# Attention scores from queries and keys in two float32r parts, one score product of 50 rows per head, maxima in pairs

## What is computed

```python
qkv = (x @ qkv_w + qkv_b).reshape(Bx, Tx, 3, H, HD).transpose(2, 0, 3, 1, 4)
q, k, v = (qkv[0], qkv[1], qkv[2])
...
q = _apply_rotary(q, rope)
k = _apply_rotary(k, rope)
scale = HD ** (-0.5)
scores = jnp.einsum('bhqd,bhkd->bhqk', q, k) * scale
causal_mask = jnp.triu(jnp.ones((Tx, Tx), dtype=bool), 1)
scores = jnp.where(causal_mask, -jnp.inf, scores)
attn = jax.nn.softmax(scores, axis=-1)
out = jnp.einsum('bhqk,bhkd->bhqd', attn, v)
```

## Time and profile before

| | |
|---|---|
| median of 3 runs | 3247.66 us |
| lowest and highest | 3235.09 and 3250.77 us |
| span of the profiled execution, first to last instruction | 3061.1 us |
| PE, PEld busy | 2843.4 (93%), 1573.9 (51%) us |
| DVE busy | 2242.9 us (73%) |
| ACT busy | 1779.3 us (58%) |
| POOL busy | 1253.7 us (41%) |

### The profile page before, as it was taken

One profiled execution on the slowest core, in us unless ns is written; L12 is line 12 of the kernel. 1 busy time (PEld: TensorE's weight loads), 2 busy tenths in 40 slices (PEclk: granted clock), 3 DMA queues, 4 the chain that ended last, 5 costly groups with the idle time before them and its releaser, 6 DMA issues.

```text
span 3061.1 us, 61038 instructions
## 1 busy us (share of the span) xinstructions
PE 2843.4 (93%) x22500; PEld 1573.9 (51%) x22500; DVE 2242.9 (73%) x5047; ACT 1779.3 (58%) x2736; POOL 1253.7 (41%) x1557
## 2 busy tenths in 40 slices
PE   7888799999999999989999999987999999999997
PEld 4433333333433334433333333323888999999997
DVE  7888788888888888899998888822393225566477
ACT  2422466666566665656665566665556666666533
POOL 6766311213521114521114765554305753443176
PEclk9999899999999999999999999998999999999998
DMA  4854323313312322412323535245336765665486
GB/s 163 209 142 106 110 56 65 66 42 76 101 39 56 66 63 59 109 43 37 66 63 91 141 94 123 89 129 152 117 93 204 233 202 175 187 183 173 136 238 193
DMA packets 290690, 359.05 MB, mean 117 GB/s; under 512 B 65404, under 2 KB 243212, under 8 KB 290140
## 3 DMA queue, kind: packets, MB, share of 16 engines
q1 hardware_dynamic: 259516, 279.94, 33.8%
q0 software_dynamic: 26112, 71.34, 7.7%
q10 hardware_dynamic: 4768, 3.88, 0.5%
HBM read 206.25 MB, written 139.21 MB: 113 GB/s over the span
## 4 chain that ended last, share of the span: by engine, by line
PE 49%; ACT 13%; DVE 10%; POOL 7%; issue 7%; DMA 2%; ACTq 1%; POOLq 0%; SPq 0%; DVEq 0%
ACT P L1643 13%; PE PB L1165 10%; PE PB L1092 8%; PE PB L1181 7%; DVE mx L1460 6%; PE PB L1062 6%; PE PB L1039 6%; PE PB L1075 5%; POOL x_slots L1846 4%; PE PB L1106 2%; PE PB L1150 2%; ACTq L1652 1%; POOL yg L1859 1%; PE PB L1129 1%; POOL x_slots L1838 1%
## 5 line engine op out<-in xcount | busy, mean ns | idle before, releaser
L1460 DVE TENSOR_REDUCE mx<-PB 128x1 f32<-128x512 f32 (+3 forms) x2560 | 1406.9, 603 | 214.6 <-PE PB L1039 135.6
L1643 ACT ACTIVATE P<-PB 128x1024 f32<-128x1024 f32 (+3 forms) x1280 | 1095.4, 894 | 643.3 <-PE PB L1075 629.3
L1039 PE MATMUL PB<-KO,QO 64*128 64x512 bf16 (+3 forms) x2560 | 762.0, 353 | 61.5 <-DVE mx L1460 51.5
L1092 PE MATMUL PB<-P,V 128*17 128x512 f32 (+3 forms) x5120 | 599.2, 540 | 11.8 <-POOL P L1797 11.7
L1062 PE MATMUL PB<-QO,KO 64*128 64x512 bf16 (+3 forms) x2560 | 546.8, 353 | 60.0 <-ACT P L1643 33.0
L1039 PEld LDWEIGHTS PB<-KO,QO 64*128 64x128 bf16 x2560 | 203.5, 94 | 718.0 <-DVE mx L1460 533.0
L1075 PE MATMUL PB<-QO,KO 34*128 34x512 bf16 (+3 forms) x2560 | 520.0, 351 | 0.6 <-DMA QO<-nh 0.4
L1797 POOL TENSOR_SCALAR_AFFINE_SELECT P<-P 128x256 f32<-128x256 f32 x512 | 208.6, 414 | 678.8 <-ACT P L1643 673.1
L1165 PE MATMUL PB<-xT,ws 128*128 128x128 f32 x3432 | 433.7, 277 | 7.1 <-ACT xT L1726 7.0
L1165 PEld LDWEIGHTS PB<-xT,ws 128*128 128x128 f32 x3432 | 408.2, 193 | 9.7 <-ACT xT L1726 9.7
L1571 DVE TENSOR_TENSOR haT<-sl,PB 64x128 f32<-64x128 f32 x350 | 101.4, 290 | 411.8 <-ACT sl L1735 407.3
(11 more groups left out here) (178 smaller groups left out, 3218.7 us busy)
## 6 DMA issues: line engine op xcount, KB each, us to landing
xq<-x_slots SPq DMA_DIRECT2D x286, 128.0 KB, 2.8
qk_parts<-pt SPq DMA_DIRECT2D x192, 128.0 KB, 2.4
KO<-qk_parts SPq DMA_DIRECT2D x192, 128.0 KB, 4.1
y_slots<-yo SPq DMA_DIRECT2D x191, 128.0 KB
QO<-qk_parts SPq DMA_DIRECT2D x64, 256.0 KB, 3.4
rden<-rden_rows SPq DMA_DIRECT2D x256, 64.0 KB
y_slots<-mx SPq DMA_DIRECT2D x95, 128.0 KB
v_rows<-vst SPq DMA_DIRECT2D x16, 544.0 KB, 4.0
```

The costliest lines, as they stand in the source:

```text
L1039: mm = pe.matmul(PB[:, bank, 0:n], QO[half, k3, j, 128 * t:128 * t + 128], KO[half, k3, j, 512 * kc:512 * kc + n], start=True, stop=True)
L1092: mm = pe.matmul(PB[32 * j:32 * j + 17, 7, c0:512], V[:, g % 2, kt, 17 * j:17 * j + 17], P[:, pbuf(g, i, j // 2), j % 2, 0:n], start=kt == ...
L1460: dve.tensor_reduce(mx[:, j, t, kc:kc + 1], PB[:, u.bank[item], 0:n], AX.X, ALU.max).then_inc(s["mx"], 1)
L1643: act.activation(P[:, pbuf(g, i, p), :, 0:n], PB[:, 2 * p:2 * p + 2, 0:n], ACT.Exp, scale=0.25).then_inc(s["exp"], 1)
```

## The change

Queries and keys are kept as two f32 parts, "high", rounded to float32r by ScalarE, and "low", what GpSimd's one subtraction leaves. The third part, `pe_` and its steps are gone. In `QO` and `KO` a head has 48 rows of products (high by high, high by low, low by high), and two rows more for the negated maximum and the ones. "sa" and "sb" become one product "s" over 50 rows of half of the array; "max" is one product over 48 rows. Both read float32r. The tensors take the same room as before. In a step the maxima are issued two at a time, one on each half. The masking products stay in bf16.

```diff
+HIGH, LOW = 0, 1
 LOADS = [(z, 64 * odd + row, odd, k, n) for odd in (0, 1)
-         for z, row, k, n in ((0, 0, 0, 2), (0, 32, 0, 2), (1, 0, 0, 1), (1, 16, 0, 1), (1, 32, 1, 1), (1, 48, 1, 1))]
-LOADS += [(z, 64 - 64 * odd + row, odd, k, 1) for odd in (0, 1) for z, row, k in ((0, 0, 2), (0, 16, 0), (1, 0, 0), (1, 16, 2))]
+         for z, row, k, n in ((1, 0, HIGH, 2), (0, 16, HIGH, 2), (1, 32, HIGH, 1), (0, 0, HIGH, 1))]
+M_ROW = 48
 NL = len(LOADS)
...
-        if k == 4 and c > 1:
-            o("lo", c - 2)
+        if k == 4 and c > 0:
+            o("lo", c - 1)
...
         quota = (want - done) // 2 * 2
         at = done
         ahead = order[n + 1] if n + 1 < len(order) else None
+        o("s", g, i, 2)
+        o("s", g, i, 3)
+        o("exp", g, i, 1)
         if len(pend) == 2:
             values(*pend.pop(0))
-        maxima(at + (quota + 2) // 4)
-        o("sa", g, i, 3)
-        o("sa", g, i, 2)
         maxima(at + quota // 2)
         if ahead:
-            o("sa", *ahead, 0)
-            o("sa", *ahead, 1)
-        o("sb", g, i, 3)
-        o("sb", g, i, 2)
-        o("exp", g, i, 1)
+            o("s", *ahead, 0)
+            o("s", *ahead, 1)
+            o("exp", *ahead, 0)
         if i >= 2:
             pumped(pumps)
-        maxima(at + quota // 2 + (quota + 2) // 4)
-        if ahead:
-            o("sb", *ahead, 0)
-            o("sb", *ahead, 1)
         maxima(at + quota)
-        if ahead:
-            o("exp", *ahead, 0)
         send_rows()
...
-    parts_d = scratch("qk_parts", [B, H, 2, 3, HD, T], BF16)
+    parts_d = scratch("qk_parts", [B, H, 2, 2, HD, T])
...
-        QO = A("QO", [128, 3, 4, T], BF16)
+        QO = A("QO", [128, 3, 2, T], F32)
         ko_at = A.at
-        KO = A("KO", [128, 3, 4, T], BF16)
+        KO = A("KO", [128, 3, 2, T], F32)
         v_at = A.at
...
+        QR, KR = QO[:, :, :, :].bitcast(F32R), KO[:, :, :, :].bitcast(F32R)
...
+                    q.wait_ge(s["c_p"], 3)
+                    for k in (0, 2):
+                        for odd in (0, 64):
+                            sync.dma_start(KO[odd + M_ROW:odd + M_ROW + 2, k], KO[odd + 32:odd + 34, 2]).then_inc(s["l_one"], 16)
...
-                    q.wait_ge(*lo_done[c])
+                    q.wait_ge(s["p_low"], c + 1)
-                        for k in range(3):
+                        for k in (HIGH, LOW):
                             for half in (0, 1):
                                 sync.dma_start(parts_d[b, :, z, k, 8 * half:8 * half + 8, tok:tok + 512],
                                                pt[w][:, k, 2 * z + half, :]).then_inc(s[f"w_p{w}"], 16)
...
-                    sync.dma_start((QO, KO)[z][row:row + 16 * n, k3, odd:4:2, :],
+                    sync.dma_start((QO, KO)[z][row:row + 16 * n, k3],
                                    parts_d[b, h0 + odd:h0 + 4:2, z, k:k + n].rearrange("h k d t -> (k d) h t")
...
-                    half = slice(64 * (j % 2), 64 * (j % 2) + 64)
-                    mm = pe.matmul(PB[:, bank, 0:n], QO[half, k3, j, 128 * t:128 * t + 128], KO[half, k3, j, 512 * kc:512 * kc + n],
-                                   start=True, stop=True)
+                    half, rows = slice(64 * (j % 2), 64 * (j % 2) + 64), slice(64 * (j % 2), 64 * (j % 2) + M_ROW)
+                    mm = pe.matmul(PB[:, bank, 0:n], QR[rows, k3, j // 2, 128 * t:128 * t + 128],
+                                   KR[rows, k3, j // 2, 512 * kc:512 * kc + n], start=True, stop=True)
                     if kc == t // 4:
...
-                elif name == "sa":
+                elif name == "s":
                     g, i, j = at
                     c, kt = STEPS[i]
                     k3, p = (g + 2) % 3, j // 2
                     n, c0 = nb(i)
                     q0 = 512 * c + c0
-                    rows = slice(64 * (j % 2), 64 * (j % 2) + 64)
+                    rows = slice(64 * (j % 2), 64 * (j % 2) + M_ROW + 2)
                     q.wait_ge(s[f"l_g{k3}"], 16 * NL * (g // 3 + 1))
+                    q.wait_ge(s[f"w_nm{p}"], 64 * (g + 1))
+                    if g:
+                        q.wait_ge(s["l_att"], 80)
                     if o.n("exp", g, i, p) > 2:
                         q.wait_ge(s["exp"], o.n("exp", g, i, p) - 2)
-                    pe.matmul(PB[:, j, 0:n], KO[rows, k3, j, 128 * kt:128 * kt + 128], QO[rows, k3, j, q0:q0 + n],
-                              start=True, stop=False).then_inc(s["sa"], 1)
-                elif name == "sb":
-                    g, i, j = at
-                    c, kt = STEPS[i]
-                    k3, p = (g + 2) % 3, j // 2
-                    n, c0 = nb(i)
-                    q0 = 512 * c + c0
-                    rows = slice(64 - 64 * (j % 2), 98 - 64 * (j % 2))
-                    q.wait_ge(s["sa"], o.n("sa", g, i, j))
-                    q.wait_ge(s[f"w_nm{p}"], 64 * (g + 1))
-                    if g:
-                        q.wait_ge(s["l_att"], 112)
-                    pe.matmul(PB[:, j, 0:n], KO[rows, k3, j, 128 * kt:128 * kt + 128], QO[rows, k3, j, q0:q0 + n],
-                              start=False, stop=True).then_inc(s["st"], 1)
+                    pe.matmul(PB[:, j, 0:n], KR[rows, k3, p, 128 * kt:128 * kt + 128], QR[rows, k3, p, q0:q0 + n],
+                              start=True, stop=True).then_inc(s["st"], 1)
...
-                elif name == "lo" and (at[0] < OWN or at[0] > 13):
-                    (c,) = at
-                    w = c % PT_
-                    q.wait_ge(s["p_mid"], c + 1)
-                    dve.tensor_tensor(pt[w][:, 2], pe_[:, c % 2], pt[w][:, 1], ALU.subtract).then_inc(s["lo_v"], 1)
...
-                    dve.tensor_copy(nh[:, p, 0, :], PB[0:32, bank, 0:128]).then_inc(s["nh"], 1)
+                    dve.tensor_copy(nh[0:32, p, :].bitcast(F32R), PB[0:32, bank, 0:128]).then_inc(s["nh"], 1)
                     q.wait_ge(s["nh"], n)
-                    dve.tensor_tensor(nh[:, p, 1, :], PB[0:32, bank, 0:128], nh[:, p, 0, :], ALU.subtract).then_inc(s["nl"], 1)
+                    dve.tensor_tensor(nh[32:64, p, :], PB[0:32, bank, 0:128], nh[0:32, p, :], ALU.subtract).then_inc(s["nl"], 1)
...
-                    act.activation(pt[w][:, 0], r[:, :, :], ACT.Copy).then_inc(s["p_hi"], 1)
-                elif name == "lo":
-                    (c,) = at
-                    q.wait_ge(s["p_rest"], c + 1)
-                    act.activation(pt[c % PT_][:, 1], pe_[:, c % 2], ACT.Copy).then_inc(s["p_mid"], 1)
+                    if c == PT_ - 1:
+                        q.wait_ge(s["m_gate"], 1)
+                        q.wait_ge(s["w_mod"], 16)
...
-                        for k in (0, 1):
-                            row = (96, 32)[j] + k
-                            act.dma_start(QO[row:row + 1, k3, 2 * p + j, :].rearrange("o (t q) -> o t q", q=128),
-                                          nh[16 * j:16 * j + 16, p, k, :]).then_inc(s[f"w_nm{p}"], 16)
+                        for k in (HIGH, LOW):
+                            row = 64 * j + M_ROW + k
+                            act.dma_start(QO[row:row + 1, k3, p, :].rearrange("o (t q) -> o t q", q=128),
+                                          nh[32 * k + 16 * j:32 * k + 16 * j + 16, p, :]).then_inc(s[f"w_nm{p}"], 16)
...
-                    q.wait_ge(s["m_gate"], 1)
-                    q.wait_ge(s["w_mod"], 16)
-                    if c >= 2:
-                        q.wait_ge(*lo_done[c - 2])
-                    pool.tensor_tensor(pe_[:, c % 2], r[:, :, :], pt[c % PT_][:, 0], ALU.subtract).then_inc(s["p_rest"], 1)
...
-                elif name == "lo" and not (at[0] < OWN or at[0] > 13):
-                    (c,) = at
-                    w = c % PT_
-                    q.wait_ge(s["p_mid"], c + 1)
-                    pool.tensor_tensor(pt[w][:, 2], pe_[:, c % 2], pt[w][:, 1], ALU.subtract).then_inc(s["lo_g"], 1)
+                    pool.tensor_tensor(pt[c % PT_][:, LOW], r[:, :, :], pt[c % PT_][:, HIGH], ALU.subtract).then_inc(s["p_low"], 1)
```

68 lines of the change are left out of this document (29 added, 39 removed).

## The result

The changed kernel takes **3678.87 us**, the median of 4 runs (3644.34 to 3699.95), against 3241.38 us of the kernel before beside it (4 runs, 3231.15 to 3250.77). The ratio is 1.131, 95% interval 1.1246 to 1.1374; it leaves out the run of 3699.95 us, which fell into a slower state of the chip. The forecast, 3135 us and faster, was wrong in sign, and the time lies 404 us above the top of its range.

What follows compares the result with a forecast made beforehand. Matrix engine and VectorE were taken to stand close together in attention, neither full, holding each other up. Terms -100 + 12 - 12 - 8 - 5 = -113 us gave 3135 us, range 3045 to 3275.

Steps and rivals of the forecast that it cites:

- The base: Whole kernel: 186.6 us lie between the profiled span of 3061.1 us and the median of 3247.7, and stay.
- (2): Attention with maxima: the new order shortens a full step from 2.67 to 2.50 us; -100 us, bounds 0 and -159.
- (1): Attention's score products: one float32r pass at 0.22 us a pair, one product instead of two; frees 0.44 us a full step.
- rival (a): Matrix engine in attention: float32r weight loads, 193 against 94 ns, come into the open; 3210 us, chance 0.15.
- rival (b): Matrix engine in attention: float32r products on two halves of the rows don't run side by side; about 3355 us, chance 0.12.
- (3): Group boundaries in attention: score products wait for the transfer of the negated maxima; +12 us, 0 to +45.
- (4): Last piece of attention, without maxima: one product instead of two ahead of each exp; -12 us, 0 to -25.
- (5): First stage: subtractions and copies removed, -8 us in the early chunks and -5 at the stage's end.
- (6): Part transfers: fewer, larger stores and fewer load issues of the same bytes, hidden by the group's own time; 0.
- (c): Score products and maxima: float32r makes four passes, 4.5 us a step; 4230 us, chance 0.04.
- (d): Attention: the boundary wait costs +45 us and the pair order gains nothing; 3267 us, chance 0.07.

Runs made afterwards that it cites:

- bf16_ops: Changed kernel with score products and maxima both reading only the upper 16 bits of each part as bf16: 3142.51 us, 1.0266 of the kernel before.
- scores_late: Changed kernel with the score pair of heads 2 and 3 and its exp moved from ahead of the value products to behind the first maxima pair: 3319.11 us, 1.0273.
- old_bf16: Changed kernel in nearly the step order of the kernel before, scores and maxima read as bf16 from the upper 16 bits: 3010.34 us, 0.9826.
- max16_old: Changed kernel in nearly the step order of the kernel before, maxima alone read as bf16, scores in float32r: 3037.83 us, 0.9933.
- the filled kernels: One useless bf16 product added ahead of each score product, in the changed kernel (3329.4 us) and in its version with bf16 scores and maxima (3174.2 us).
- the second chip: The unaltered changed kernel run again on another chip beside the kernel before: 3468.86 against 3066.54 us, 1.131.

## Why the prediction was wrong, point by point

**The base.** The forecast took 186.6 us as lying around the profiled execution. They don't: the changed kernel's profiled execution took 3687.9 us with a span of 3686.2, so only 1.7 us lie outside the span. The page of before has 936 us of experts; on the chip of the timed runs the changed kernel's experts take 1110.6. The kernel before itself ran at 3064 us on one chip and at 3223 on another. The forecast itself was not hurt: it added its sum to the measured 3247.7 us, and the ratio of the two kernels is 1.131 on both chips.

**(2) The replay of the order, -100 us, is the step that failed, and the clock that it ran at is the other.** Measured in the nearest pure form (bf16, one product) the order costs +134 us in the stretch, some 64 of them at full clock by the estimate above. The replay had the parts right, and set each at its best: VectorE on the first pair at 0.39 (measured 0.53), the second product of pair B at 1.1 (1.28), values at 1.5 (1.94), next pair at 2.5 (2.92). In bf16_ops, where the loads are short, the same points stand at 0.43, 1.18, 1.74 and 2.72 (538.93 to 541.65 us of its trace), so about half of the error is the order's and half the bare loads'. It found VectorE idle 0.06 to 0.1 us, so a slack of nothing. In such a step every 0.1 us of delay is 0.1 us of step, and I gave the delays no price and no sign; the range's bound for this term was 0, never above. What scores_late shows could be read in the list of the changed step ahead of the prediction: a score pair stands between a maximum that waits and the value products.

**(1) The score product.** One pass was right, one record each, and so was 0.22 us a pair, as far as loads are covered: 0.23 us from 600.69 to 600.92. It is 0.34 us only behind a wait (600.35 to 600.69, against 0.24 in bf16_ops), which is the bare load of rival (a) and not the halves of rival (b). The gain of dropping a product is real where it stands alone (old_bf16, 0.9826).

**Rival (a), the bare weight loads, was the right mechanism with the wrong place and price.** I asked whether loads would fill the array's time, and found room. They cost elsewhere, some 0.2 us a full step at full clock (2.69 against 2.50, 2.92 against 2.72): a product that waits for a bank has its load behind that wait, bare, and VectorE waits at its end. The earlier trace rows had the count: 689 waits for VectorE ahead of these loads between 440 and 1900 us. With the 99 ns between the two loads of the earlier trace rows that is 68 us in this window alone; max16_old measured 118 us in all. I had argued it away by the experts, where products stream without such a wait. The rule that I cited there, from the Trainium skill ("TensorE: Matmul & The Clock Gate", Weight-path perf modes), that fast weight load is off for FP32, fits float32r as well: 182 to 187 ns a load against 94.

**The clock was missing altogether, and it is the largest term.** The earlier trace rows had 0.99 for attention, and I held it there without a word. It fell to 0.77 and 0.80, with 970 and 809 us at half clock where before had 28. Some 280 of the 398 us of lost stretch hang on it, by the steps at the two levels; the filled kernels show 154 of them, the part by which it makes order and type dearer together.

**(3) The boundary wait, +12 us: right in size.** The score products waited for the rows of the maxima 13.6 us in all, 24 times (0.4 us, once, in the kernel before); the forecast counted what VectorE loses by that, and no run shows how much of it reached the time:

```profile
  DMA QO<-nh: 13.6, 24
```

**(4) Attention without maxima, -12 us: right**, 113.9 to 100.9 us, although the clock fell there too (0.93 to 0.85).

**(5) The first stage, -13 us: wrong in sign.** The first score product came 13.6 us later (354.5). With bf16 maxima it comes at 338 to 344 us in the eight kernels that have them (340.9 before), so the removed subtractions gained next to nothing, and the float32r maxima lose some 13. VectorE is busy 15 us less there, and that was not its bound.

**(6) Transfers, 0**: nothing in the waits speaks against it.

**Rivals (b), (c), (d).** (c) is out by the records. Of the rivals' times (b)'s, 3355, is nearest to what came, but by luck: its point of decision, a pair dearer than 0.39, was not reached. (d) named the new order as a risk, yet priced it at the gain of (2) lost and 45 us of waiting, with a chance of 0.07. In stretch of the second chip: one product less -36, order +134, float32r +111, the two together +189 more. That these give 398 is how the square is made, and no check. Put at full clock by the estimates above: one product less -72, order +64, float32r +80, the two together +44, and the clock +282. The +44 have no experiment of their own.

**What stays open.** Why the clock falls as it does can't be told from these runs, only that it was at half for longest in the kernel with both the new order and float32r, and came back when useless products were added. Nor was it tried to keep float32r maxima and hide their loads.

## What to carry to other kernels

In a step in which two engines take turns, list what stands on the matrix engine between a product that waits and the next thing the other engine needs; move work from behind that wait to ahead of it. A product that waits has its weight load bare, so price a slower load by the number of waits, not by the array's room. Where a replay finds no slack, its error has one sign: give it a price above zero. Look at how long the kernel stands at half clock, too: a small delay in each step cost here some 115 us by itself and some 280 more by the clock. And a maximum that only shifts an exponent can be computed in the cheapest type.

## What the runs showed of the hardware that was not expected

- A float32r product streams in one pass like bf16 (0.39 us for 512 columns either way at full clock), but its weight load is twice as long: median 183 to 187 ns against 93 for 128 columns.
- Behind a wait the load is bare: after a float32r pair on two halves of the rows that had waited, the next starts 0.34 us later (bf16_ops: 0.24). Where the loads are covered it is 0.23 us in either type.
- The granted clock is 1.00 or 0.50 and nothing between. The same full step of the changed kernel takes 2.92 us at one and 4.56 at the other, and its eight records of value products hold the array 0.98 and 1.83 us.
- The granted clock in attention, on the mean: 0.99 before, 0.80 in the changed kernel, 0.96 with 2400 records more of useless bf16 products, which made it 140 us faster. In the bf16 kernel the same filling raised the clock from 0.91 to 0.99 and gained nothing, as a full step gets 0.2 us longer by it at full clock.
- The same kernel's experts stage took 938.7 us on one chip and 1110.6 on another, at clocks of 0.98 and 0.92.
